# Gated delta-rule attention: state update through a weighted k, z kept token-major, three steps on other engines, and a new order on every engine

## The chip, the cores and the metric

The program runs on one core of a Trainium2 chip. A core has five engines that run their own instruction streams and meet through semaphores: TensorE (PE, matrix products; its weight loads are shown apart as PEld), VectorE (DVE), ScalarE (ACT), GpSimd (POOL) and SyncE (SP, which here only issues DMAs). The metric is the device time of one execution in microseconds (us); less is better.

## The reference

One transformer layer with eight samples of 512 tokens and 256 channels: modulation and LayerNorm, a gated delta-rule attention with 16 key heads and 32 value heads of width 128, and a mixture of experts. Nearly all time goes to the attention, which in essence is this:

```python
qkvz  = h @ W_qkvz.T                      # q, k, v go through a causal 4-tap convolution and silu; z does not
decay = tril(exp(g_i - g_j))              # g: cumulated log gates inside a chunk
T     = inverse(I - A);  A = -strict_tril((k*beta) @ k.T * decay)
for each chunk:                           # state starts at 0, one 128 x 128 matrix per value head
    v_new = T @ (v*beta) - (T @ (k*beta*exp(g))) @ state
    out   = (q*exp(g)) @ state + tril(q @ k.T * decay) @ v_new
    state = state*exp(g_last) + (k*exp(g_last - g)).T @ v_new
y = (norm_weight * (rmsnorm(out) * silu(z))) @ W_out.T
```

## The kernel before

There are three parts, one after the other: `modulation_and_gates`, `attention`, `experts`. The change lies in `attention`.

A **step** is one sample and one key head with its two value heads: 128 steps. The kernel works with chunks of 128 tokens, so a step has four chunks and eight units (chunk times value head). Each engine runs a loop whose body is written out by hand in a table (`PE_ORDER`, `ACT_ORDER`, `DVE_ORDER`, `POOL_ORDER`). An entry such as `Y2@3` means: task Y, part 2, of the step that is three ahead of the loop's count. One pass of the body does every task once, for steps up to four ahead; this software pipeline is the only thing that sets the order. Each engine takes its entries strictly in that order, and a wait that is not met holds all that stands behind it. `loop` runs the partly filled passes at the ends, and a register loop of two passes for the rest.

The tasks, with the lines of the kernel before:

- `P0` to `P11` (PE, L658): the projection, six tiles of 128 columns (k, q, v, v, z, z), two products each into two PSUM banks by turns. `C` (ACT, L886) and `T0` to `T11` (DVE, L1018): the convolution. `SK`, `SQ`, `SV`, `Z` (ACT): silu.
- `KT`, `QT`, `VT` (PE) transpose to token-major. `KN`, `QN` (ACT square, DVE sum), `PW` (POOL root) and `SM`, `SN` (DVE) give the norms' factors; `w_c` holds the weight of each token in the state update.
- `GL` (POOL, L1194): adds a constant table `bound` (0 or -1e30) to the gate rows; `GE` (ACT, L924): the decay as exp. `KK` (PE, L690), `GA` (DVE, L1072): the matrices A and attn of all units. `SL` (POOL, L1203) puts -1 on A's diagonal.
- The **ladder** inverts the 64 x 64 blocks of all eight units by doubling. A rung n is `M` (PE, L718), `q` (DVE, L1085), `Y` (PE, L725), `y` (DVE, L1093), `X` (DVE, L1102, a transpose) and `XB` (half on ACT, L936, half on POOL, L1225), and the next `Y` needs this `XB`. It begins with `AB` (DVE, L1078), `L` (PE, L713), `y0` (DVE, L1090), and has five rungs. `s`, `XD`, `Q6`, `p6` (DVE, L1113), `Z6`, `YC`, `XC` join the blocks, and `D`, `F`, `RL`, `G`, `v`, `W`, `IV` refine the inverse.
- The **state chain** of a step: `KS` (PE, L803, k against state), `RR` (DVE, L1129), `TR` (PE, L816), then `VX` (ACT, L979, the copy `vx`) and `VW` (DVE, L1140, the same product times `w_c`), `U` (PE, L826, k_tok against `vw`), `ST` (DVE, L1151), `SD` (POOL, L1239) and `O` (PE, L837 and L838).
- The end of a step: `OT`, `OQ` (ACT), `OS` (DVE), `OP`, `ON` (POOL, L1244 and L1253: the RMS factor and its product with the output), `ON` (PE, L852, a transpose), `HT` (DVE, L1164: times norm_weight and z), `OY` (PE, L868), `YA` (DVE, L1170).

SyncE loads weights and gate rows one to four steps ahead; before each load it waits for the last reader of the buffer.

Of the kernel before, what the change touches and what calls it, by code (L numbers as in the profile page):

```python
# [33 lines left out]
PE_ORDER = ("M2@3 ON1@1 O0@2 VT0@3 Y2@3 KS1@2 W1@2 M3@3 TR1@2 P0@4 Y3@3 U1@2 P1@4 M4@3 KS2@2 O1@2 P2@4 Y4@3 TR2@2 "  # L34
            "P3@4 M5@3 VT1@3 O2@2 U2@2 P4@4 KS3@2 Y5@3 P5@4 KT@4 QT@4 XD@3 Q6@3 TR3@2 P6@4 Z6@3 P7@4 D0@3 O3@2 XC@3 "
            "D1@3 KK0@4 KK1@4 P8@4 OY0@1 OY1@1 G0@3 L@4 P9@4 W0@3 M1@4 P10@4 TR0@3 Y1@4 G1@3 P11@4 U0@3 ON0@2")
ACT_ORDER = ("GE@2 OT3@0 C3@2 OQ3@0 XC@1 SV0@2 AO@2 v0@1 IV0@1 XB1@2 VX0@1 v1@1 SV1@2 XB2@2 OT0@1 Z0@2 Z1@2 XB3@2 "
             "IV1@1 VK0@2 VX1@1 C0@3 XB4@2 OT1@1 OQ0@1 VX2@1 C1@3 OQ1@1 XB5@2 OT2@1 VK1@2 OQ2@1 SK@3 SQ@3 C2@3 KN@3 "
             "QN@3 XD@2 VX3@1 KT@3 YC@2")
DVE_ORDER = ("T10@3 y0@3 T11@3 X1@3 q1@3 YA1@0 VW0@2 y1@3 X2@3 ST0@2 HT0@1 q2@3 HT1@1 y2@3 RR1@2 X3@3 q3@3 VW1@2 "  # L40
# [1606 lines left out]
```

## Time and profile before

| | before |
|---|---|
| median of 3 runs | 4839.93 us (4837.36 to 4840.07) |
| profiled execution, span from first to last instruction | 4831.3 us |
| PE busy | 4671.0 us, 97% |
| DVE busy | 4411.5 us, 91% |
| ACT busy | 3467.6 us, 72% |
| POOL busy | 2743.0 us, 57% |
| DMA engines | 377.26 MB moved, queue busy 24.7% |

The span of the profiled execution is 8.6 us under the median. Attention fills it from about 118 us to 4665 us. A matrix product's duration in the trace includes the time it takes to drain, in which the next one already runs; a busy share of PE therefore tells less than the distance from one start to the next. The same holds in a small measure on the other engines, where an instruction often starts some 0.1 us before the end of the one in front.

### The profile page before, as it was taken

To read this page: it belongs to the slowest core of one execution; us is meant where nothing else is said; L and a number is where in the kernel's file an instruction comes from. 1 tells how busy PE (TensorE), PEld (TensorE's weight loads), DVE (VectorE), ACT (ScalarE), POOL (GpSimd) and SP (SyncE) were. 2 spreads that over 40 slices of the span, in tenths; PEclk is the share of its full clock that TensorE was granted. 3 is DMA by queue.
4 is the path that set the end of the run, shared out by engine and by line. 5 is a ranking of instruction groups with operands and counts; after the bars stand their busy time and mean duration, and the time that the engine had idled before them with its cause. 6 is when DMAs were issued, how large, how long until landed. Compare 5 with 4: busy or idle time off the path is not lost. (4 is left out here: it accounts for less than half of the span.)

```text
span 4831.3 us, 132942 instructions
## 1 busy us (share of the span) xinstructions
PE 4671.0 (97%) x38533; PEld 3195.1 (66%) x38788; DVE 4411.5 (91%) x9152; ACT 3467.6 (72%) x8336; POOL 2743.0 (57%) x2329
## 2 busy tenths in 40 slices
...
DMA packets 185165, 377.26 MB, mean 78 GB/s; under 512 B 86400, under 2 KB 95744, under 8 KB 184960
## 3 DMA queue, kind: packets, MB, share of 16 engines
q1 hardware_dynamic: 185088, 376.46, 24.7%
...
q8 instruction: 20, 0.33, 0.0%
...
## 5 line engine op out<-in xcount | busy, mean ns | idle before, releaser
L658 PE MATMUL p_proj<-hid,w_in 128*128 128x512 f32 x3072 | 1626.7, 612 | 30.0 <-POOL ident_h L1185 28.9
L1018 DVE SCALAR_TENSOR_TENSOR conv<-p_proj,taps,conv 128x509 f32<-128x509 f32 (+2 forms) x1536 | 1134.8, 739 | 48.2 <-ACT conv L886 34.9
L1199 POOL TENSOR_TENSOR root<-sums,half_pow 128x8 f32<-128x8 f32 x128 | 210.8, 1647 | 862.9 <-DVE sums L1028 843.9
L1225 POOL TENSOR_SCALAR_AFFINE_SELECT x_bd<-x_t 128x512 bf16<-128x512 bf16 x640 | 422.6, 660 | 213.5 <-DVE x_t L1102 211.2
L658 PEld LDWEIGHTS p_proj<-hid,w_in 128*128 128x128 f32 x3072 | 497.3, 192 | 55.1 <-POOL ident_h L1185 29.1
L1093 DVE TENSOR_TENSOR y_h<-p_lev,y_h 128x512 bf16<-128x512 f32 x640 | 440.2, 688 | 74.4 <-PE p_lev L725 74.4
L868 PE MATMUL p_out<-h_t,w_out 128*128 128x512 f32 x1024 | 476.5, 608 | 2.2 <-DVE h_t L1164 1.1
L936 ACT ACTIVATE x_bd<-x_t 64x512 bf16<-64x512 bf16 x640 | 397.7, 621 | 96.3 <-DVE x_t L1102 96.2
L1102 DVE STREAM_TRANSPOSE x_t<-y_h 128x512 bf16<-128x512 bf16 x640 | 450.3, 704 | 4.5
L1072 DVE SCALAR_TENSOR_TENSOR ga<-p_out,neg_c,dec 128x256 f32<-128x256 f32 x1024 | 412.9, 477 | 35.4 <-ACT dec L924 34.8
L886 ACT ACTIVATE conv<-p_proj,taps 128x512 f32<-128x512 f32 x512 | 351.7, 687 | 121.9 <-PE p_proj L658 119.3
L1085 DVE TENSOR_TENSOR q_h<-p_lev,consts 128x512 bf16<-128x512 f32 x640 | 429.6, 671 | 3.8 <-PE p_lev L718 3.8
L979 ACT ACTIVATE vx<-p_b 128x256 f32<-128x256 f32 x512 | 197.9, 386 | 285.8 <-PE p_b L816 161.4
L1217 POOL TENSOR_TENSOR r_lo<-resid 128x1024 bf16<-128x1024 f32 x128 | 242.3, 1893 | 247.9 <-DVE resid L1118 247.9
L838 PE MATMUL p_b<-vx,ga 128*128 128x128 f32 x2048 | 375.1, 275 | 0.0
L868 PEld LDWEIGHTS p_out<-h_t,w_out 128*128 128x128 f32 x1024 | 184.6, 190 | 285.0 <-DVE ga L1072 147.9
L725 PEld LDWEIGHTS p_lev<-q_h,x_bd 128*128 128x128 bf16 x5120 | 216.5, 97 | 213.5 <-issue 101.5
L985 ACT ACTIVATE o_tok<-p_b 128x256 f32<-128x256 f32 x512 | 194.1, 379 | 199.5 <-PE p_b L838 196.4
L718 PEld LDWEIGHTS p_lev<-y_h,a_bd 128*128 128x128 bf16 x5120 | 222.7, 98 | 152.1 <-issue 84.2
L1232 POOL TENSOR_TENSOR q_dec<-kq,e_row 128x512 f32<-128x512 f32 x256 | 320.0, 1271 | 0.0
L924 ACT ACTIVATE dec<-low,g_neg 128x128 f32<-128x128 f32 x1024 | 313.3, 388 | 1.6
L1244 POOL TENSOR_TENSOR o_sc<-o_sc,neg_half 128x8 f32<-128x8 f32 x128 | 211.4, 1651 | 168.9 <-DVE o_sc L1159 168.9
...
## 6 DMA issues: line engine op xcount, KB each, us to landing
w_in<-in_w_in SPq DMA_DIRECT2D x128, 768.0 KB, 6.3
g_row<-rows_scratch SPq DMA_DIRECT2D x128, 512.0 KB, 3.2
hid<-h_scratch SPq DMA_DIRECT2D x128, 512.0 KB, 7.4
e_row<-exp_rows_scratch SPq DMA_DIRECT2D x128, 512.0 KB, 5.3
w_out<-in_w_out SPq DMA_DIRECT2D x128, 256.5 KB, 2.7
...
```

The costliest lines, as they stand in the source:

```text
L658: last = pe.matmul(p_proj[tile % 2][:], w_in[p][:, kt, tile * P:(tile + 1) * P], hid[p][:, kt, :], start=(kt == 0), stop=(kt == KT - 1))
L838: last = pe.matmul(p_b[:, at], ga[p][:, n * HD + h, 1, :], vx[:, h, :], start=(n == 0), stop=True)
L868: last = pe.matmul(p_out[n][:], w_out[p][:, h * D + n * P:h * D + (n + 1) * P], h_t[:, :, h, :], start=(h == 0), stop=(h == HD - 1))
L886: act.activation(conv[:, n, :], p_proj[n % 2][:], ACT.Copy, scale=taps[p][:, n, PAD:PAD + 1])\
L936: act.activation(x_bd[0:HB, :, 0:HB], x_t[0:HB], ACT.Copy).then_inc(s["xbd"], 1)
L1018: dve.scalar_tensor_tensor(conv[:, tile, late:], p_proj[tile % 2][:, 0:S - late], taps[p][:, tile, j:j + 1], conv[:, tile, late:], ALU.mul ...
L1072: last = dve.scalar_tensor_tensor(ga[p][:, u], kk, neg_c[p][:, n, h:h + 1], each(dec[:, u, :], 2), ALU.mult, ALU.mult)
L1085: dve.tensor_tensor(q_h[:], levels(), each(const["mask"][:, n * HB:(n + 1) * HB], U), ALU.mult)\
L1093: dve.tensor_tensor(y_h[:], levels(), y_h[:], ALU.add).then_inc(s["y_done"], 1)
L1102: dve.transpose(x_t[:].rearrange("p u f -> p (u f)"), y_h[:].rearrange("p u f -> p (u f)"))\
L1225: pool.affine_select(x_bd[:, :, HB:P], x_t[:], [[0, U], [0, HB]], ALU.is_ge, zero, base=-HB, channel_multiplier=1).then_inc(s["xbd_low"], 1)
L1232: last = pool.tensor_tensor(q_dec[p][:, :, h, :], kq[p][:, :, 1, :], e_row[p][:].rearrange("p (c h) i -> p c h i", h=HD)[:, :, h, :], ALU. ...
```

## The change

- **Weighted k.** `VW` is gone. A new task `KW` on POOL makes `k_w` = k_tok times `w_c` for chunks 0 to 2 and both heads, 768 elements per partition. `U` takes `vx` itself and is two products of 128 columns in place of one of 256.
- **z token-major.** `P8` to `P11` have the hidden states of one chunk as the stationary operand and 256 columns of weights as the moving one: two products of 256 columns each, where one of 512 was. `ON` on POOL gets a second instruction that multiplies the output by z. `HT` has only norm_weight left to apply; it moves from DVE to ACT as a scaled copy.
- **Half product on ScalarE.** `p6` on DVE becomes `PH` on ACT.
- **Causal bound.** `GL` is an affine_select with fill -1e30; the constant table `bound` is gone.
- **Orders.** All four tables are new, and the lists of who frees a PSUM bank follow them. Most steps are now at most three ahead, and the end of a step falls in its own pass.

```diff
-PE_ORDER = ("M2@3 ON1@1 O0@2 VT0@3 Y2@3 KS1@2 W1@2 M3@3 TR1@2 P0@4 Y3@3 U1@2 P1@4 M4@3 KS2@2 O1@2 P2@4 Y4@3 TR2@2 "
+PE_ORDER = ("U0@1 Y1@2 P11@2 O0@1 M2@2 KS1@1 P0@3 Y2@2 TR1@1 P1@3 M3@2 U1@1 O1@1 KS2@1 Y3@2 VT0@2 P2@3 TR2@1 M4@2 P3@3 U2@1 "
...
+        k_w = two("k_w", [P, NC - 1, HD, DH])
...
-                    last = pe.matmul(p_proj[tile % 2][:], w_in[p][:, kt, tile * P:(tile + 1) * P], hid[p][:, kt, :],
-                                     start=(kt == 0), stop=(kt == KT - 1))
+                    if tile < 4:
+                        ...
+                    else:
+                        c = n - 4 * KT
+                        for k in range(KT):
+                            last = pe.matmul(p_proj[tile % 2][:, kt * HD * DH:(kt + 1) * HD * DH],
+                                             hid[p][:, k, c * CH:(c + 1) * CH], w_in[p][:, k, 4 * P:6 * P],
+                                             start=(k == 0), stop=(k == KT - 1))
...
                 elif name == "U":
-                    t.wait(pe, "vw_done", n + 1)
+                    t.wait(pe, "vx_done", n + 1)
-                        t.wait(pe, "k_tok_done")
+                        t.wait(pe, "kw_done")
-                    pe.matmul(p_a[:, HD * DH:2 * HD * DH], k_tok[p][:, n, :], vw[:].rearrange("p h f -> p (h f)"),
-                              start=True, stop=True).then_inc(s["u_mm"], 1)
+                    for h in range(HD):
+                        last = pe.matmul(p_a[:, (HD + h) * DH:(HD + h + 1) * DH], k_w[p][:, n, h, :], vx[:, h, :],
+                                         start=True, stop=True)
+                    last.then_inc(s["u_mm"], 1)
...
+                elif name == "PH":
+                    t.wait(act, "q6_mm")
+                    t.wait(act, "z6_mm", back=1)
+                    act.activation(p_h[HB:P], p_lev[HB:P, :].rearrange("p (u f) -> p u f", f=HB), ACT.Copy).then_inc(s["p6_done"], 1)
...
                 elif name == "VX":
-                    if n < NC - 1:
-                        t.wait(act, "vw_done", n + 1)
+                        t.wait(act, "u_mm", n)
...
+                elif name == "HT":
+                    t.wait(act, "on_mm", n + 1)
+                    t.wait(act, "y_out", back=1)
+                    act.activation(cols(h_t, n), bank(n), ACT.Copy, scale=const["norm_w"]).then_inc(s["h_done"], 1)
...
-                elif name == "p":
-                    dve.tensor_copy(p_h[HB:P], levels()[HB:P]).then_inc(s["p6_done"], 1)
...
-                elif name == "VW":
-                    dve.tensor_tensor(vw[:], p_b[:, 0:HD * DH].rearrange("p (h f) -> p h f", h=HD),
-                                      over(w_c[p][:, n, :], [P, HD, DH]), ALU.mult).then_inc(s["vw_done"], 1)
...
-                elif name == "HT":
-                    dve.scalar_tensor_tensor(cols(h_t, n), bank(n), const["norm_w"], cols(z_t[p], n),
-                                             ALU.mult, ALU.mult).then_inc(s["h_done"], 1)
...
-                    pool.tensor_tensor(low[:], g_row[p][:], each(const["bound"], U), ALU.add).then_inc(s["g_low"], 1)
+                    pool.affine_select(low[:], g_row[p][:], [[0, U], [1, CH]], ALU.is_ge, far_below, base=0,
+                                       channel_multiplier=-1).then_inc(s["g_low"], 1)
...
+                elif name == "KW":
+                    t.wait(pool, "k_tok_done")
+                    t.wait(pool, "w_scaled")
+                    t.wait(pool, "u_mm", back=2)
+                    pool.tensor_tensor(k_w[p][:], k_tok[p][:, 0:NC - 1].unsqueeze(2).to_broadcast([P, NC - 1, HD, DH]),
+                                       w_c[p][:, 0:NC - 1].unsqueeze(3).to_broadcast([P, NC - 1, HD, DH]), ALU.mult)\
+                        .then_inc(s["kw_done"], 1)
...
                     pool.tensor_tensor(o, o, scale, ALU.mult).then_inc(s["o_nrm"], 1)
+                    t.wait(pool, "o_nrm", 1)
+                    t.wait(pool, "z_done")
+                    pool.tensor_tensor(o, o, z_t[p][:].rearrange("p c h f -> p (c h) f"), ALU.mult).then_inc(s["o_nrm"], 1)
```

POOL, before, from `XB` of rung 1 to `AL` (a_lo) in one pass of the loop; the four rows of x_bd are `XB` of rungs 1 to 4. Rows that only hold a wait or count in a register are left out here and below:

```order
L1225 AFFINE_SELECT x_bd<-x_t 128x8x64 [waits at_y_mm]
L1253 TENSOR_TENSOR o_tok<-o_tok,o_sc 128x1024 [waits at_ot_done]
L1225 AFFINE_SELECT x_bd<-x_t 128x8x64 [waits at_xt_done,at_y_mm]
L1239 TENSOR_TENSOR state_dec<-state,g_exp 128x256 [waits fed_g0]
L1194 TENSOR_TENSOR low<-g_row,consts 128x1024 [waits at_decay]
L1225 AFFINE_SELECT x_bd<-x_t 128x8x64 [waits at_xt_done,at_y_mm]
L1232 TENSOR_TENSOR q_dec<-kq,e_row 128x4x128 [waits at_o_mm,fed_e1,at_q_act]
L1232 TENSOR_TENSOR q_dec<-kq,e_row 128x4x128
L1225 AFFINE_SELECT x_bd<-x_t 128x8x64 [waits at_xt_done,at_y_mm]
L1209 TENSOR_TENSOR a_rest<-ga 128x1024 [waits at_d_mm]
L1239 TENSOR_TENSOR state_dec<-state,g_exp 128x256 [waits at_st_done]
L1213 TENSOR_TENSOR a_lo<-a_rest 128x1024 [waits at_d_mm,at_rest]
```

The same stretch now, from rung 1 to rung 4:

```order
L1224 AFFINE_SELECT x_bd<-x_t 128x8x64 [waits at_xt_done,at_y_mm]
L1259 TENSOR_TENSOR o_tok<-o_tok,o_sc 128x1024 [waits at_ot_done]
L1262 TENSOR_TENSOR o_tok<-o_tok,z_t 128x1024 [waits at_z_done,at_o_nrm]
L1245 TENSOR_TENSOR state_dec<-state,g_exp 128x256 [waits fed_g0,at_st_done]
L1224 AFFINE_SELECT x_bd<-x_t 128x8x64 [waits at_xt_done,at_y_mm]
L1231 TENSOR_TENSOR q_dec<-kq,e_row 128x4x128 [waits at_o_mm,fed_e1,at_q_act]
L1231 TENSOR_TENSOR q_dec<-kq,e_row 128x4x128
L1224 AFFINE_SELECT x_bd<-x_t 128x8x64 [waits at_xt_done,at_y_mm]
L1192 AFFINE_SELECT low<-g_row 128x1024 [waits at_decay]
L1245 TENSOR_TENSOR state_dec<-state,g_exp 128x256 [waits at_st_done]
L1208 TENSOR_TENSOR a_rest<-ga 128x1024 [waits at_d_mm,at_alo,at_strict]
L1224 AFFINE_SELECT x_bd<-x_t 128x8x64 [waits at_xt_done,at_y_mm]
```

Between rungs 1 and 2 there are now the two long products of the normalisation; q_dec, which stood before rung 4, stands before rung 3, and a_rest before rung 4 has `GL` and the second `SD` with it.

DVE, before, from the `y` of rung 4 (y_h) up to that of rung 5; conv is a tap, x_t the transpose `X`, q_h the mask `q`:

```order
L1093 TENSOR_TENSOR y_h<-p_lev,y_h 128x512 [waits at_y_mm]
L1140 TENSOR_TENSOR vw<-p_b,w_c 128x256 [waits at_u_mm,at_tr_mm]
L1102 STREAM_TRANSPOSE x_t<-y_h 128x512 [waits at_xbd_low,at_xbd,at_y_done]
L1018 SCALAR_TENSOR_TENSOR conv<-p_proj,taps,conv 128x511 [waits at_tap0]
L1085 TENSOR_TENSOR q_h<-p_lev,consts 128x512 [waits at_y_mm,at_q_mm]
L1018 SCALAR_TENSOR_TENSOR conv<-p_proj,taps,conv 128x509 [waits at_conv_done]
L1151 TENSOR_TENSOR state<-p_a,state_dec 128x256 [waits at_o_mm,at_sdec,at_u_mm]
L1018 SCALAR_TENSOR_TENSOR conv<-p_proj,taps,conv 128x510 [waits at_tap1]
L1018 SCALAR_TENSOR_TENSOR conv<-p_proj,taps,conv 128x511 [waits at_tap1]
```

DVE now, from the `y` of rung 4 to that of rung 5:

```order
L1109 TENSOR_TENSOR y_h<-p_lev,y_h 128x512 [waits at_y_mm]
L1033 SCALAR_TENSOR_TENSOR conv<-p_proj,taps,conv 128x509 [waits at_conv_done]
L1118 STREAM_TRANSPOSE x_t<-y_h 128x512 [waits at_xbd_low,at_xbd,at_y_done]
L1101 TENSOR_TENSOR q_h<-p_lev,consts 128x512 [waits at_y_mm,at_q_mm]
L1033 SCALAR_TENSOR_TENSOR conv<-p_proj,taps,conv 128x510 [waits at_tap1]
L1033 SCALAR_TENSOR_TENSOR conv<-p_proj,taps,conv 128x511 [waits at_tap1]
L1109 TENSOR_TENSOR y_h<-p_lev,y_h 128x512 [waits at_y_mm]
```

Before the `y` of rung 5 there stand six instructions now, where nine stood: vw is gone, and one tap and the state's update have moved to earlier rungs.

## Rows read from the trace of the kernel before

**Rows 1.** Busy time by engine over 58 passes; columns as the header says.

```profile
core 0: us, PE busy (x) PEld busy (x) DVE busy (x) ACT busy (x) POOL busy (x), PEclk, DMA share, GB/s
1010.93:3044.85 2033.92, 2017.70 (x17172) 1397.76 (x17286) 1940.12 (x4060) 1530.90 (x3713) 1231.63 (x1044) 1.00 0.25 77
```

**Rows 2.** PE over time: start, length, engine, line, operation, tiles, shape, count.

```profile
2403.18 0.63 PE L706 MATMUL p_out<-consts,v_t 128*128 128x128 f32 x4
2403.65 0.39 PE L837 MATMUL p_b<-state,q_dec 128*128 128x128 f32 x2
...
2404.55 0.60 PE L826 MATMUL p_a<-vw,k_tok 128*128 128x256 f32 x2
2404.98 1.02 PE L658 MATMUL p_proj<-hid,w_in 128*128 128x512 f32 x2
2405.84 0.59 PE L803 MATMUL p_a<-state,kq 128*128 128x256 f32 x2
2406.27 0.40 PE L725 MATMUL p_lev<-q_h,x_bd 128*128 128x64 bf16 x8
2406.50 1.10 PE L658 MATMUL p_proj<-hid,w_in 128*128 128x512 f32 x2
...
2411.67 0.22 PE L764 MATMUL p_out<-y_dn,ga 128*128 128x128 bf16 x1
...
2412.34 0.44 PE L837 MATMUL p_b<-state,q_dec 128*128 128x128 f32 x2
...
2417.28 3.70 PE L868 MATMUL p_out<-h_t,w_out 128*128 128x512 f32 x8
2420.82 0.39 PE L780 MATMUL p_out<-x_dn,resid 128*128 128x128 bf16 x4
```

**Rows 3.** Groups by line of what leaves DVE: count, busy us, mean ns, idle before.

```profile
L1140 DVE TENSOR_TENSOR vw<-p_b,w_c 128x256 f32<-128x256 f32 x384 | 159.7, 416 | 14.3 <-PE p_b L816 7.4
L1164 DVE SCALAR_TENSOR_TENSOR h_t<-p_out,norm_w,z_t 128x512 f32<-128x512 f32 x256 | 191.1, 747 | 8.7 <-PE p_out L852 3.3
L1113 DVE CAST p_h<-p_lev 64x512 bf16<-64x512 f32 x128 | 88.9, 694 | 4.6 <-PE p_lev L737 0.7
```

**Rows 4.** Groups by line on ACT: a scaled copy of 512, a half copy.

```profile
L886 ACT ACTIVATE conv<-p_proj,taps 128x512 f32<-128x512 f32 x512 | 351.7, 687 | 121.9 <-PE p_proj L658 119.3 <-issue 2.6
L945 ACT ACTIVATE y_dn<-p_lev 64x512 bf16<-64x512 f32 x128 | 75.8, 592 | 3.5 <-PE p_lev L743 0.3
```

**Rows 5.** Groups by line on POOL: products, selects and the root.

```profile
L1232 POOL TENSOR_TENSOR q_dec<-kq,e_row 128x512 f32<-128x512 f32 x256 | 320.0, 1271 | 0.0
L1194 POOL TENSOR_TENSOR low<-g_row,consts 128x1024 f32<-128x1024 f32 x128 | 302.3, 2362 | 0.2 <-POOL ident_h L1185 0.2
L1253 POOL TENSOR_TENSOR o_tok<-o_tok,o_sc 128x1024 f32<-128x1024 f32 x128 | 242.7, 1896 | 0.2
L1203 POOL TENSOR_SCALAR_AFFINE_SELECT ga<-ga 128x1024 f32<-128x1024 f32 x128 | 140.4, 1097 | 229.9 <-DVE ga L1072 229.9
L1199 POOL TENSOR_TENSOR root<-sums,half_pow 128x8 f32<-128x8 f32 x128 | 210.8, 1647 | 862.9 <-DVE sums L1028 843.9 <-DVE sums L1024 19.0
```

**Rows 6.** DVE and POOL over time, a transpose and its POOL half.

```profile
2426.09 0.71 DVE L1102 STREAM_TRANSPOSE x_t<-y_h 128x512 bf16<-128x512 bf16 x1
2426.99 0.66 POOL L1225 TENSOR_SCALAR_AFFINE_SELECT x_bd<-x_t 128x512 bf16<-128x512 bf16 x1 [0.51 <-DVE x_t L1102]
```

**Rows 7.** DVE over time: tap, RR, y, tap, q, tap, state, taps.

```profile
2401.04 0.74 DVE L1018 SCALAR_TENSOR_TENSOR conv<-p_proj,taps,conv 128x510 f32<-128x510 f32 x1
2401.76 0.69 DVE L1093 TENSOR_TENSOR y_h<-p_lev,y_h 128x512 bf16<-128x512 f32 x1
...
2404.55 0.73 DVE L1018 SCALAR_TENSOR_TENSOR conv<-p_proj,taps,conv 128x509 f32<-128x509 f32 x1
2405.20 0.42 DVE L1151 TENSOR_TENSOR state<-p_a,state_dec 128x256 f32<-128x256 f32 x1
2405.53 1.53 DVE L1018 SCALAR_TENSOR_TENSOR conv<-p_proj,taps,conv 128x510 f32<-128x510 f32 x2
```

118 lines of the change are left out of this document (56 added, 62 removed), and 3 rows, old and new, of the table DVE_ORDER.

## Prediction

> **What bounds the kernel now.** I read the busy time by engine first, then PE and DVE over time, then the groups by line. The middle of the attention repeats itself: [rows 1] hold 58 passes (4060 DVE instructions, 70 a pass) in 2033.92 us at a granted clock of 1.00, so a pass takes 35.07 us, and 128 of them are 4489 us of the 4831.3 us span. Everything hangs on the length of a pass. In one pass DVE is busy 1940.12/58 = 33.45 us, ACT 26.4, POOL 21.2. PE shows 34.8, but that counts drains. From start to start [rows 2] a projection pair takes 0.86 us, four transposes 0.45, a 256-column product 0.43, eight 64-column products 0.23, the four products of one O 0.90 (twice 0.45), a half of `D` 0.67, and the eight rows of `OY` 3.54. One pass of PE is then: twelve P 10.3; six transposes 2.6; `KK` 1.7; `OY` 3.5; three `KS` and three `U` 2.6; four `TR` 1.8; four `O` 3.1; fourteen groups of 64 columns 3.2; `XD` 0.5; `D` 1.3; `G` 0.4; `W` 1.8 (each half is a `D` half and an identity product of 0.21). The sum is 32.9 us. So PE waits for 2.2 us of a pass and DVE for 1.6: DVE is the bound by a hair, and PE stands right behind it. That caps what relief of DVE can give.
>
> **The change part by part.** Off DVE go three `VW`, two `HT` and `p6`: (159.7 + 191.1 + 88.9)/128 = 3.4 us a pass [rows 3]. DVE falls to 30.0 us busy, and PE with its 32.9 becomes the bound.
>
> PE's columns stay the same: `P8` to `P11` are eight products of 256 where four of 512 were, and each `U` is two of 128. The trace has no projection with 256 columns. Between the bounds of nothing (512 columns in 0.43 a row, 256 columns in 0.215, the same rate [rows 2]) and 0.06 per P as the extra weight load shows itself, I take 0.2 us a pass for both edits: floor 33.1.
>
> ACT gets two `HT`, scaled copies of 512 from PSUM like L886, 0.69 each, and `PH`, 0.59 like L945 [rows 4]: 26.4 + 2.0 = 28.4 us. No new function set comes in, all three are copies.
>
> POOL: `GL` falls from 2.36 to a select of 1024 elements, 1.10 in the row of `SL` [rows 5]. The product with z reads two full fp32 tiles, as L1194 does, so 2.36 and not the 1.90 of L1253, whose second operand is one number per 128; its other end is q_dec's 1.27 for 512, that is 2.54. `KW` has 768 elements: 1.42 by L1253's rate, to which its weight operand is nearest, 1.9 by q_dec's. I take 1.5. POOL is at 21.2 - 1.3 + 2.4 + 1.5 = 23.8 us. Sums alone say nothing against this; the orders do.
>
> The GPSIMD Engine Reference of the Trainium skill (section 4.1, Engine selection) sends elementwise products of two tensors to VectorE, since GpSimd takes about twice as long. The price agrees with the rows of L1194 and L1253; as a rule for this kernel I set it aside, since the time on POOL is only paid where somebody waits for it. Its section 1 also says that GpSimd shares its SBUF interfaces with VectorE, which would lengthen POOL's products beside DVE work; that is among the rivals.
>
> **The new orders, walked with row durations.** I follow the ring of dependences that closes after one pass. It starts at `L`, the ladder's first product.
>
> By PE, from `L` to `U1`: `L`, P9, `G1`, `W0`, M1, `W1`, `TR0`, P10, `U0`, Y1, P11, `O0`, M2, `KS1`, P0, Y2, `TR1`, P1, M3: 9.85 us by the distances above. Then `U1` 0.60, and on DVE from `ST1` on without a gap: `ST1`, T0, T1, `RR2`, y3, X4, q4, T2, `ST2`, y4, T3, X5, q5, T4, T5, up to y5. A tap takes 0.66 from start to start, 0.79 when the next needs its result, y 0.61, a state update 0.33 [rows 7], together 9.2 us. That is 19.7 from `L` to y5.
>
> By POOL, from `L`: 0.2 until `OS1` is done, root 1.65, its factor 0.3, XB1 0.63, both normalisation products 4.3, `SD` 0.6, XB2 0.65, q_dec 2.5, XB3 0.63, `GL` 1.05, `SD` 0.6, a_rest 1.85, XB4 0.65: 15.6 us [rows 5, 6]. An XB starts 0.2 after its X ends. Y4 and y4 follow, 0.4, and T3, X5, q5, T4, T5 with y4 3.95: 19.95 to y5. The two ways are equal within 0.3. What `GL` loses in length, the z product takes up; without it this way would be the bound.
>
> From y5 back to `L`: T5 ends as y5 starts; on ACT `SQ`, C2, `OT2`, `PH`, `XD`, `KT`, `QN` 4.25; the DVE sum 0.68; the root on POOL 1.85; `SM0` to `SM3` with `F1` between them 1.5; `GA` 3.2; `SL` 1.25; `AB` 0.95 with the hand-over: 13.7 us. `KW` stands before `SL` on POOL; after `F1` it and `RL` take 0.2 + 1.9 + 1.5 = 3.6 against `GA`'s 3.6, so it hides, and at 1.9 it would cost 0.3.
>
> The ring is 19.95 + 13.7 = 33.7 us. With 0.2 for the split products and 0.15 for near misses of `KW` and of Y2 behind XB2 I take **34.05 us a pass**, 1.0 over PE's floor. The waits on PE should lie before `L` (on `AB`), before `D0` (on `YC`), and at Y2 and Y4.
>
> SyncE loses nothing: the gate factors follow the same step's last `YA`, now 6 us before `SD1` needs them. The ends of the loop keep their length but for the last normalisation, with the z product of 2.4 us in the open. The other parts are unchanged; the missing table is nothing beside 377 MB.
>
> Sum: 4831.3 - 128 x (35.07 - 34.05) + 2.4 = 4703; with the 8.6 us by which the median stands over the span, 4712.
>
> **Rivals.**
>
> 1. *PE reaches its floor.* If real hand-overs are a little shorter than my ring or the slack lies elsewhere, a pass is 33.1 to 33.5: 4831.3 - 128 x 1.8 + 11 = 4612. For it: the ring exceeds the floor by only 0.6 before surcharges. Against it: PE lost 2.2 us a pass when its partner DVE was full, and four engines are dense now.
> 2. *The waits stay.* PE's 2.2 us are hand-overs of an in-order ladder and not the wait for a full DVE; then a pass is 33.1 + 1.9 = 35.0 and the time about 4840. For it: DVE too lost 1.6 us though it was the bound.
> 3. *A slower ladder.* The five rungs now stand 3.5 us apart where 2.8 is the least (y 0.69, X 0.70, a hand-over of 0.2, XB 0.66, Y and its hand-overs 0.5), and a 1.9 to 2.5 us product stands before three of the XBs on POOL. If XB3, XB4 and XB5 each miss by 0.5 more than in my walk, the pass is 35.5: 4831.3 + 128 x 0.45 + 11 = 4900. It decides from 0.35 a rung on.
> 4. *POOL's products stretch* through the shared interfaces. Eight products come to some 15 us; a tenth more puts 0.9 on the POOL way: 35.0 a pass, about 4830. Against it: they are alike in mean whether large or small [rows 5], and DVE was 95% busy beside them.
>
> **How the numbers follow.** The forecast (33.6 to 34.6 a pass, 4655 to 4785) has 0.62, rival 1 0.14, rivals 2 and 4 together 0.15, rival 3 0.09. The range of 4640 to 4795 takes in `KW` at its dear end (4750) and leaves some 0.2 outside. A difference under 0.2%, 10 us, can't be told from no change. Faster takes the forecast, rival 1 and most of the middle cases: 0.86; same 0.04; slower 0.10.
>
> **What would show it.** DVE near 30.0 us busy of a pass, POOL near 23.8, ACT near 28.4. PE's gaps should fall from 2.2 to about 1.1 us a pass, and the z product and `KW` last 2.36 and 1.4 to 1.9. The forecast is wrong if POOL is idle before each XB and the pass is still long, if ACT holds up `VX` or `XB`, or if the 256-column products run slower than 0.43 a pair.

## The result, and the profile after

The changed kernel is slower: median 5039.4 us (5038.2 to 5041.7, 4 runs) against 4838.7 us (4836.2 to 4840.1, 4 runs) in the same job, a ratio of 1.0416 [1.0401, 1.0431]. The forecast was 4712, with a range of 4640 to 4795. The profiled execution has a span of 5038.3 us.

From the windows of the changed kernel, 54 passes between two first products `L`; the columns are those of [rows 1]:

```profile
core 0: us, PE busy (x) PEld busy (x) DVE busy (x) ACT busy (x) POOL busy (x), PEclk, DMA share, GB/s
1016.57:2999.30 1982.73, 1884.45 (x16850) 1403.56 (x16850) 1769.13 (x3456) 1539.77 (x3618) 1283.01 (x1080) 1.00 0.23 73
```

A pass takes 36.72 us where it took 35.07. DVE is busy 32.8 us of it, PE 34.9, ACT 28.5, POOL 23.8. ACT and POOL are where the prediction put them (28.4 and 23.8). DVE is not: 30.0 were expected. So 2.8 us of DVE's time are something else than the work that was counted. The groups by line, of the whole execution, show 2.2 of them; the rest is taken up below. First what was priced ahead (columns as in [rows 3]):

```profile
L1262 POOL TENSOR_TENSOR o_tok<-o_tok,z_t 128x1024 f32<-128x1024 f32 x128 | 302.0, 2359 | 10.0
L1238 POOL TENSOR_TENSOR k_w<-k_tok,w_c 128x768 f32<-128x768 f32 x128 | 188.0, 1469 | 0.0
L1192 POOL TENSOR_SCALAR_AFFINE_SELECT low<-g_row 128x1024 f32<-128x1024 f32 x128 | 139.2, 1087 | 3.1 <-issue 2.7 <-POOL ident_h L1182 0.4
L1001 ACT ACTIVATE h_t<-p_out,norm_w 128x512 f32<-128x512 f32 x256 | 172.0, 673 | 10.5 <-PE p_out L859 10.5
L957 ACT ACTIVATE p_h<-p_lev 64x512 bf16<-64x512 f32 x128 | 75.8, 592 | 3.1
```

These answer [rows 4, 5]: the z product lasts 2.36 us, `KW` 1.47, the select 1.09, `HT` 0.67 and `PH` 0.59. All were as forecast. Then three groups in which the loss shows:

```profile
L1061 DVE SCALAR_TENSOR_TENSOR neg_c<-cc,inv 128x8 f32<-128x8 f32 x128 | 239.8, 1874 | 4.4
L1068 DVE TENSOR_TENSOR w_c<-neg_c,g_col 128x8 f32<-128x8 f32 x128 | 79.3, 619 | 0.0
L898 ACT ACTIVATE z_t<-p_proj 128x512 f32<-128x512 f32 x256 | 150.6, 588 | 112.1 <-POOL o_tok L1262 112.0 <-PE p_proj L664 0.2
```

`neg_c` (task `SM3`) has eight numbers per partition. In the profile before it took 21.3 us in all, 167 ns each; now it takes 1874 ns. `w_c` (`SN0`) went from 156 ns to 619. The arithmetic and the shapes of both are the same. The third line is a plain wait: `Z` on ACT waits for the second product of `ON`, 0.9 us a pass.

DVE over time in the changed kernel, start and length first:

```profile
2411.59 0.17 DVE L1049 TENSOR_SCALAR neg_n<-root 128x8 f32<-128x8 f32 x1 [0.37 <-POOL root L1198]
2411.80 0.20 DVE L1053 RECIPROCAL inv<-neg_n 128x8 f32<-128x8 f32 x1
2411.92 0.68 DVE L1130 TENSOR_TENSOR resid<-p_out,consts 128x512 f32<-128x512 f32 x1
2412.52 0.16 DVE L1058 TENSOR_TENSOR cc<-inv,g_col 128x8 f32<-128x8 f32 x1
2412.71 1.89 DVE L1061 SCALAR_TENSOR_TENSOR neg_c<-cc,inv 128x8 f32<-128x8 f32 x1
2414.79 3.23 DVE L1088 SCALAR_TENSOR_TENSOR ga<-p_out,neg_c,dec 128x256 f32<-128x256 f32 x8 [0.19 <-DVE neg_c L1061]
```

POOL over the same time:

```profile
2412.68 1.89 POOL L1216 TENSOR_TENSOR r_lo<-resid 128x1024 bf16<-128x1024 f32 x1 [1.12 <-DVE resid L1130]
2414.53 1.47 POOL L1238 TENSOR_TENSOR k_w<-k_tok,w_c 128x768 f32<-128x768 f32 x1
2418.18 1.10 POOL L1202 TENSOR_SCALAR_AFFINE_SELECT ga<-ga 128x1024 f32<-128x1024 f32 x1 [2.18 <-DVE ga L1088]
```

`neg_c` begins 0.03 us after `r_lo` and ends with it, while `r_lo` keeps its normal 1.89 us. Before, `F1` stood behind `SM3`. These rows are DVE and then POOL of the kernel before:

```profile
2414.36 0.17 DVE L1046 SCALAR_TENSOR_TENSOR neg_c<-cc,inv 128x8 f32<-128x8 f32 x1
2414.47 0.69 DVE L1118 TENSOR_TENSOR resid<-p_out,consts 128x512 f32<-128x512 f32 x1
2415.07 0.16 DVE L1052 TENSOR_TENSOR w_c<-neg_c,g_col 128x8 f32<-128x8 f32 x1
```

```profile
2415.24 1.89 POOL L1217 TENSOR_TENSOR r_lo<-resid 128x1024 bf16<-128x1024 f32 x1 [1.79 <-DVE resid L1118]
```

`neg_c` was over 0.7 us before `r_lo` started. The new order has `F1` between `SM1` and `SM2`; that releases `r_lo` just as `neg_c` is due. And `neg_c` opens `GA`, the head of the chain to `L`.

### The profile page after: what moved, and what is told of

It reads as the page before. It is cut to its first block and busy times, and to the rows that moved or that the text cites. A ratio compares the mean times of both kernels' runs of the same rounds, so it can differ in the third digit from the quotient of the medians.

```text
span 5038.3 us, 136395 instructions
## 1 busy us (share of the span) xinstructions
PE 4684.8 (93%) x40580; PEld 3441.5 (68%) x40580; DVE 4319.1 (86%) x8384; ACT 3736.8 (74%) x8718; POOL 3066.3 (61%) x2585
## 5 line engine op out<-in xcount | busy, mean ns | idle before, releaser
L659 PE MATMUL p_proj<-hid,w_in 128*128 128x512 f32 x2048 | 1110.6, 624 | 54.3 <-POOL ident_h L1182 28.8
L1109 DVE TENSOR_TENSOR y_h<-p_lev,y_h 128x512 bf16<-128x512 f32 x640 | 438.3, 685 | 260.7 <-PE p_lev L733 260.7
L664 PE MATMUL p_proj<-w_in,hid 128*128 128x256 f32 x2048 | 552.1, 392 | 1.0 <-DVE conv L1033 1.0
L1088 DVE SCALAR_TENSOR_TENSOR ga<-p_out,neg_c,dec 128x256 f32<-128x256 f32 x1024 | 412.9, 475 | 24.1 <-DVE neg_c L1061 23.8
L664 PEld LDWEIGHTS p_proj<-w_in,hid 128*128 128x128 f32 x2048 | 362.1, 192 | 35.1 <-DVE conv L1033 1.5
L659 PEld LDWEIGHTS p_proj<-hid,w_in 128*128 128x128 f32 x2048 | 310.7, 191 | 107.8 <-ACT z_t L898 73.2
L846 PEld LDWEIGHTS p_b<-vx,ga 128*128 128x128 f32 x2048 | 310.4, 192 | 6.6
L961 ACT ACTIVATE x_dn<-p_tr 64x512 bf16<-64x512 f32 x128 | 75.5, 590 | 322.3 <-PE p_tr L757 322.3
```

What stands on the lines that cost most here:

```text
L659: last = pe.matmul(p_proj[tile % 2][:], w_in[p][:, kt, tile * P:(tile + 1) * P], hid[p][:, kt, :], start=(kt == 0), stop=(kt == KT - 1))
L664: last = pe.matmul(p_proj[tile % 2][:, kt * HD * DH:(kt + 1) * HD * DH], hid[p][:, k, c * CH:(c + 1) * CH], w_in[p][:, k, 4 * P:6 * P], st ...
L846: last = pe.matmul(p_b[:, at], ga[p][:, n * HD + h, 1, :], vx[:, h, :], start=(n == 0), stop=True)
L1088: last = dve.scalar_tensor_tensor(ga[p][:, u], kk, neg_c[p][:, n, h:h + 1], each(dec[:, u, :], 2), ALU.mult, ALU.mult)
L1109: dve.tensor_tensor(y_h[:], levels(), y_h[:], ALU.add).then_inc(s["y_done"], 1)
```

## The experiments

The theory: a DVE instruction of certain forms can't run while POOL runs a large one; it is held to the end. The rivals: `F1`'s place costs by itself; `Z`'s new wait; PE or POOL bind anyway. Each kernel was run against the kernel before on the same chip. Pass lengths are the distance between first products `L` near 1000 and 3000 us of the trace, divided by the number of passes.

**1. `F1` behind `SM3`, in the changed kernel**

```diff
-SM0@3 SM1@3 F1@2 SM2@3 SM3@3 GA0@3
+SM0@3 SM1@3 SM2@3 SM3@3 F1@2 GA0@3
```

> The changed kernel with one entry of DVE_ORDER moved: F1 (the residual of the inverse, whose end releases r_lo on POOL) stands behind SM3 (neg_c) in place of between SM1 and SM2. Theory A, the held instruction: neg_c reads two SBUF tensors and is held for the whole of POOL's r_lo (1.89 us for 8 elements, where the same line took 0.17 before). Out of r_lo's way it takes 0.17 again, GA starts some 1.5 us earlier, and a pass of 36.72 us falls to 35.1 to 35.4, the time to 4830 to 4875 us. Theory B, the ladder: five rungs 3.5 us apart and z's release (ScalarE waits 0.88 us a pass for the second product) set the pass; neg_c only uses slack. Then the pass moves by less than 0.4 us and the time stays above 4985 us, whatever neg_c takes.

Measured: 4847.8 us (9 runs), ratio 1.0028 [1.0018, 1.0038]; `neg_c` 167 ns, a pass 35.22 us. One entry of one table brings back 191.6 us of the 200.7 lost.

**2. `F1` between `SM1` and `SM2`, in the kernel before**

```diff
-F0@3 SM0@4 SM1@4 SM2@4 SM3@4 F1@3 SN0@3
+F0@3 SM0@4 SM1@4 F1@3 SM2@4 SM3@4 SN0@3
```

> The kernel before with F1 moved forward between SM1 and SM2, the place it has in the changed kernel, and nothing else. Theory A: r_lo now starts as neg_c does, neg_c goes from 0.17 to about 1.9 us, on an engine that was full: the pass goes from 35.07 to 36.4 to 36.9 us and the time to 5010 to 5070 us. Theory B: nothing holds neg_c here since the new tasks on POOL and the new ladder are absent; the time stays within 20 us of before.

Measured: 5039.9 us (4 runs), ratio 1.0418 [1.0401, 1.0436]; a pass 36.69 us. The same move alone makes the kernel before as slow as the changed one. Its POOL and DVE over time:

```profile
2411.51 1.90 POOL L1217 TENSOR_TENSOR r_lo<-resid 128x1024 bf16<-128x1024 f32 x1 [1.72 <-DVE resid L1118]
2411.54 1.89 DVE L1046 SCALAR_TENSOR_TENSOR neg_c<-cc,inv 128x8 f32<-128x8 f32 x1
```

**3. z product first, in the changed kernel.** The two products of `ON` change places, and `Z` waits only for the first.

```diff
-pool.tensor_tensor(o, o, scale, ALU.mult); t.wait(pool, "z_done"); pool.tensor_tensor(o, o, z)
+t.wait(pool, "z_done"); pool.tensor_tensor(o, o, z); pool.tensor_tensor(o, o, scale, ALU.mult)
-t.wait(act, "o_nrm", back=2)
+t.wait(act, "o_nrm", 1, back=2)
```

> The changed kernel with the two products of the normalisation on POOL exchanged: times z first, then times the RMS factor, and z's silu on ScalarE waits for the first alone. z_t is free 1.9 us earlier. If the wait of ScalarE for z_t (0.88 us a pass) and the projection's wait behind it (0.4 to 0.6) are part of the loss, the wait goes, the first rungs start earlier and the pass falls by 0.3 to 0.6 us: 4960 to 5000 us. If theory A alone sets the pass, 5020 to 5040 us.

Measured: 5031.2 us (4 runs), ratio 1.0402 [1.0385, 1.0419]; a pass 36.64 us. `Z`'s idle time falls from 112 us to 0.4, but the kernel gains 8 us at most, and the intervals of the two ratios (1.0401 to 1.0431 without the edit) overlap: the wait was real and stood beside the chain.

**4. Both, and `w_c` (`SN0`) right behind `SM3`**

```diff
-SM0@3 SM1@3 F1@2 SM2@3 SM3@3 GA0@3 ... ST0@2 SN0@3 X2@3
+SM0@3 SM1@3 SM2@3 SM3@3 SN0@3 F1@2 GA0@3 ... ST0@2 X2@3
```

> The changed kernel with F1 behind neg_c, w_c (SN0, held 0.35 us by POOL's z product) right behind neg_c, and the z product first. Theory A and the z release together take back 1.65 + 0.35 + 0.4 us a pass: 34.3 us, near the ring of 34.05 us of the prediction, and 4720 to 4770 us, below both kernels. If the ladder itself is the bound (theory B), 4950 us or more.

Measured: 4827.3 us (10 runs), ratio 0.9982 [0.9972, 0.9992]; `neg_c` and `w_c` 167 ns, a pass 35.01 us. Faster than the kernel before by 0.2%, but 0.7 us a pass over what I expected. So these three edits take back the whole loss against the kernel before, and experiment 1 alone takes back most of it; that the gain did not come has other causes (experiments 7, 8 and 12). One of them is a new held instruction: `OS` part 0 (`o_sc`, eight elements, two SBUF inputs) now falls beside `KW` and takes 372 ns in the median, where it took 156 in the changed kernel. DVE, then POOL:

```profile
2414.91 0.37 DVE L1159 TENSOR_TENSOR o_sc<-o_ss,q_s 128x8 f32<-128x8 f32 x1
```

```profile
2413.79 1.47 POOL L1238 TENSOR_TENSOR k_w<-k_tok,w_c 128x768 f32<-128x768 f32 x1
```

**5. `neg_c` with one SBUF input.** In the changed kernel, four `tensor_scalar` of two columns each.

```diff
-dve.scalar_tensor_tensor(neg_c[p][:], cc[:], -1.0, inv_k, ALU.mult, ALU.mult)
+for c in range(NC):
+    dve.tensor_scalar(neg_c[p][:, c, :], cc[:, c, :], inv[:, 0, c:c + 1], -1.0, ALU.mult, ALU.mult)
```

> The changed kernel with its orders as they are (F1 between SM1 and SM2, r_lo released just before neg_c), only that neg_c is made by four tensor_scalar instructions of 2 columns each with one SBUF tensor input (the factor 1/norm comes as a per-partition scalar) instead of one with two. Theory (a DVE instruction with two SBUF tensor inputs is held while a two-input POOL product runs): the four are not held, together 0.4 to 0.6 us, so GA starts 1.3 us earlier than in the changed kernel, 34.9 to 35.3 us a pass, 4815 to 4865 us. Rival (it is the place of F1 that costs, for instance that neg_c waits for r_lo's memory or that the ladder is late for another reason): 5025 to 5045 us, and one of the four lasts 1.5 us.

Measured: 5367.6 us (4 runs), ratio 1.11 [1.1081, 1.1118]. The expectation failed: the kernel got slower still. DVE, then POOL:

```profile
2410.66 3.58 DVE L1062 TENSOR_SCALAR neg_c<-cc,inv 128x2 f32<-128x2 f32 x4
```

```profile
2410.63 1.89 POOL L1217 TENSOR_TENSOR r_lo<-resid 128x1024 bf16<-128x1024 f32 x1 [1.12 <-DVE resid L1131]
2412.48 1.47 POOL L1239 TENSOR_TENSOR k_w<-k_tok,w_c 128x768 f32<-128x768 f32 x1
```

The four end 0.3 us behind `k_w`. A `tensor_scalar` on fp32 in SBUF is held as well. The records of the four are 1890, 1512, 216 and 215 ns, nearly the same in 127 of 128 steps: the first is held to the end of `r_lo`, the second starts 0.02 us before `k_w` and is held to its end, and the last two are free. A pass is 39.29 us. That is 2.6 us more than in the changed kernel, of which these rows explain 1.7; the rest was not followed up. It was not `F1`'s place alone that costs, and "two inputs" was too narrow.

**6. Small DVE instructions beside known POOL instructions.** On the kernel of experiment 4, results unread.

```diff
+GA0, then tensor_scalar 128x8, then tensor_tensor 128x8   (r_lo runs)
+T8, then tensor_tensor 128x8                             (root runs)
+T9, then tensor_tensor 128x8                             (SL runs)
+q5, then tensor_tensor 128x8                             (XB5 runs)
+q1, then tensor_copy 128x128, then tensor_tensor 128x8   (z product runs)
```

> The kernel with all three order changes (F1 late, w_c right behind neg_c, z product first), plus small DVE instructions of 128x8 on constants, whose results nobody reads. Beside r_lo (two full tensors, 1.9 us): first one with one input, then one with two. Behind T8, beside the root (pow of 128x8 on POOL, 1.65 us): two inputs. Behind T9, beside SL (affine select of 1024 fp32, 1.1 us): two inputs. Behind q5, beside XB5 (select of 512 bf16, 0.66 us): two inputs. Behind q1, beside the product with z (2.37 us): a copy of 128x128 fp32, then two inputs. Theory: 'two SBUF inputs are held to the end of a POOL instruction with two inputs': one input 0.17 us, the copy 0.2 us; beside r_lo about 1.2 us, beside z 0.5 to 1.2 us, beside the root 1.2 us; beside the two selects 0.17 us. Rival a: any POOL instruction holds: SL up to 0.5, XB5 up to 0.4 us too. Rival b: only large ones hold: 0.17 us beside the root. Rival c: anything on DVE that reads SBUF is held: the copy and the one-input instruction too. The time is of no interest: some 0.5 to 2 us more a pass.

Measured, groups by line; L1051 and L1041 stand beside `r_lo`, L1043 beside the root, L1045 beside `SL`, L1047 beside `XB5`, L1053 and L1049 beside the z product:

```profile
L1053 DVE COPY junk<-consts 128x128 f32<-128x128 f32 x128 | 168.7, 1318 | 0.0
L1051 DVE TENSOR_SCALAR junk<-consts 128x8 f32<-128x8 f32 x128 | 165.4, 1292 | 0.0
L1045 DVE TENSOR_TENSOR junk<-consts 128x8 f32<-128x8 f32 x128 | 80.9, 632 | 0.0
L1047 DVE TENSOR_TENSOR junk<-consts 128x8 f32<-128x8 f32 x128 | 46.8, 366 | 0.0
L1043 DVE TENSOR_TENSOR junk<-consts 128x8 f32<-128x8 f32 x128 | 19.9, 156 | 0.0
L1049 DVE TENSOR_TENSOR junk<-consts 128x8 f32<-128x8 f32 x128 | 19.7, 154 | 0.0
L1041 DVE TENSOR_TENSOR junk<-consts 128x8 f32<-128x8 f32 x128 | 19.6, 153 | 0.0
```

Selects hold too (0.63 and 0.37 us to their ends), and a copy and a `tensor_scalar` are held: rival a is right for the selects, and part of rival c. Those that come behind a held one (L1041, L1049) take 153 and 154 ns; they start as one POOL instruction ends and just before the next begins. Beside the root nothing is held (156 ns), as rival b said, although the root lasts 1.64 us. The time was 5032 us (one run), a pass 36.65 us, 1.6 more than in experiment 4.

**7. Half of `OY` left out,** on the kernel of experiment 4: `for h in range(1)`, the second head's part of the output projection.

> The kernel with all three order changes (4827 us, 35.0 us a pass), where OY leaves out the second head's product: four instead of eight matmuls of 512 columns, 1.7 us less of PE's work in each pass, in the stretch from y5 to L where PE stands beside the chain of squares, root, neg_c, GA, SL, AB. It leaves out half of the output projection. Theory 'the ring through GA binds there': L waits for a_bd as before, 4800 to 4830 us. Rival 'PE's own sequence binds' (its distances add up to 34.6 us here and not to the 32.9 us of the estimate): 1.7 us a pass less at most, 4620 to 4700 us. Between them: both are equally long, then the gain is a few tenths a pass.

Measured: 4816.2 us (5 runs), ratio 0.9962 [0.9948, 0.9976]. 1.7 us less of PE's work a pass brought 11 us in all. PE's waits before `L`, in experiment 4 and then in experiment 7:

```profile
L721 PE MATMUL p_lev<-eye_h,a_bd 128*128 128x64 bf16 x1024 | 51.8, 194 | 12.6 <-DVE a_bd L1094 12.6
```

```profile
L788 PE MATMUL p_out<-x_dn,resid 128*128 128x128 bf16 x1024 | 99.0, 219 | 73.4 <-DVE y_acc L1167 73.4
L721 PE MATMUL p_lev<-eye_h,a_bd 128*128 128x64 bf16 x1024 | 52.5, 195 | 51.9 <-DVE a_bd L1094 51.9
```

PE now waits for `YA` (0.6 us in experiment 4) and `a_bd` instead: the chain through `GA` closes that half of the ring.

**8. Half of `P9`, `P10` and `P11` left out,** on the kernel of experiment 4 (one of two products in each sum).

> The kernel with all three order changes (4827 us), where P9, P10 and P11 leave out the second half of their sum: 2 instead of 4 matmuls of 256 columns each, together 1.3 us less of PE's work in a pass, all between L and U1, where PE has hardly a gap. It leaves out half of the z and part of the projection sum. Theory 'the ring's half from L to U1 is PE's own sequence': a pass gets shorter by what PE saves until the way by POOL (o_tok products, q_dec, XB3) binds: 0.5 to 1.2 us a pass, 4675 to 4765 us. Rival 'POOL's way already binds there' : 4800 to 4830 us.

Measured: 4817.7 us (5 runs), ratio 0.9962 [0.9948, 0.9976], against 1.3 us less of PE's work a pass. The ladder's `Y`, in experiment 4 and then in experiment 8:

```profile
L733 PE MATMUL p_lev<-q_h,x_bd 128*128 128x64 bf16 x5120 | 253.3, 193 | 3.7 <-POOL x_bd L1224 2.9
```

```profile
L734 PE MATMUL p_lev<-q_h,x_bd 128*128 128x64 bf16 x5120 | 253.3, 193 | 65.0 <-POOL x_bd L1225 63.8 <-ACT x_bd L944 1.1
```

The 61 us more are POOL's: its way (products of `ON`, q_dec, `XB`) is nearly as long as PE's. My first theory for this half was wrong, the rival right.

**9. Three exchanges on the kernel of experiment 4**

```diff
 ACT   -KT@3 QN@3              +QN@3 KT@3
 POOL  -PW@3 RL@2 KW@2 SL@3    +PW@3 KW@2 RL@2 SL@3
 DVE   -YA0@0 AB0@3 AB1@3 OS1@1   +YA0@0 OS1@1 AB0@3 AB1@3
```

> The kernel with all three order changes (4827 us, 35.0 us a pass), with three more exchanges of neighbours on the two halves of the ring. From y5 to L: QN before KT on ACT (squares 0.4 us earlier, so the root too), KW before RL on POOL (SL no longer waits 0.2 us for KW, and OS0 no longer 0.2 us), OS1 before AB0 on DVE (0.1 us on that way). From L to y5: the power on POOL starts 0.8 us earlier by OS1's new place. Theory: both halves are closed by chains without slack (14.6 us from y5 to L, 20.4 us from L to y5 by POOL and by PE alike); halving OY or P9 to P11 did not help since another chain stood beside. Then y5 to L gets 0.3 to 0.5 us shorter and L to y5 at most 0.1: 34.5 to 34.7 us a pass, 4760 to 4790 us. Rival: the chain of y5 to L ends on PE's own sequence (OY's last product), so nothing comes of it: 4815 to 4830 us. Second rival: an exchange brings a held instruction back (OS1 beside SL, or the sum beside another product): over 4840 us.

Measured: 4932.8 us (5 runs), ratio 1.0203 [1.0189, 1.0217]: the second rival in kind, a held instruction, but with a victim that it did not name. `KW` now starts as the root ends, exactly when `SM0`, a `tensor_scalar`, wants to start. DVE, then POOL:

```profile
2427.73 1.39 DVE L1049 TENSOR_SCALAR neg_n<-root 128x8 f32<-128x8 f32 x1
```

```profile
2426.03 1.64 POOL L1198 TENSOR_TENSOR root<-sums,half_pow 128x8 f32<-128x8 f32 x1 [6.15 <-DVE sums L1043]
2427.63 1.47 POOL L1238 TENSOR_TENSOR k_w<-k_tok,w_c 128x768 f32<-128x768 f32 x1
```

1390 ns in place of 171: I walked into the same trap again, with its rule half known.

**10. `neg_c` on ACT,** in the changed kernel, orders as they are but for the new entry `NC` behind `VX3`.

```diff
-dve.scalar_tensor_tensor(neg_c[p][:], cc[:], -1.0, inv_k, ALU.mult, ALU.mult)
+for c in range(NC):
+    act.activation(neg_c[p][:, c, :], cc[:, c, :], ACT.Copy, scale=inv[:, 0, c:c + 1])
```

> The changed kernel with its orders, r_lo released at the same place, only that neg_c is made on ACT: four scaled copies of 128x2 (the sign goes into cc on DVE), on an engine that does not share its SBUF access with POOL. Theory (DVE instructions whose tensors are all in SBUF are held to the end of the POOL instruction that runs; ACT's are not): the four take about 0.2 us each beside r_lo, GA starts 0.8 to 1.1 us earlier than in the changed kernel: 35.3 to 35.8 us a pass, 4860 to 4930 us. Rival (r_lo's release itself, or F1's place, costs): 5025 to 5045 us, or ACT's instructions last over 1 us beside r_lo.

Measured: 4898.9 us (4 runs), ratio 1.0137 [1.0122, 1.0153]; a pass 35.61 us. ACT over time, and POOL:

```profile
2413.33 0.85 ACT L959 ACTIVATE neg_c<-cc,inv 128x2 f32<-128x2 f32 x4 [1.99 <-DVE cc L1066]
```

```profile
2413.31 1.90 POOL L1220 TENSOR_TENSOR r_lo<-resid 128x1024 bf16<-128x1024 f32 x1 [1.12 <-DVE resid L1134]
```

The same arithmetic at the same moment beside the same `r_lo` is not held on ACT. So it is DVE's instruction that is held while POOL's runs, and not `r_lo`'s release that costs.

**11. More forms.** On the kernel of experiment 4: behind `GA0` a `reduce_sum` (128x128 to 4), a `reciprocal` (128x8) and a copy from fp32 to bf16 (128x128), behind `q1` a product of two bf16 inputs (128x8).

> The kernel with all three order changes, plus small DVE instructions on constants, to see which forms are held. Beside r_lo, in this order: a reduce_sum of 128x128 fp32 to 4, a reciprocal of 128x8 fp32, a copy of 128x128 from fp32 to bf16. Beside the product with z: a product of two bf16 inputs of 128x8. So far held: two SBUF inputs (fp32), a tensor_scalar and a copy with one fp32 SBUF input; not held: anything with a PSUM input, and the 32x32 transposes of bf16. Theory 1 (held are two SBUF inputs, and forms that DVE runs at a multiple of its rate): the sum 0.2 us and not held, the reciprocal not held, the copy held for what is left of r_lo, the bf16 product held. Theory 2 (held is everything with all tensors in SBUF but the transposes): the sum is held, about 1.1 us.

```profile
L1044 DVE TENSOR_TENSOR junk_b<-ident_h 128x8 bf16<-128x8 bf16 x128 | 161.6, 1262 | 0.0
L1042 DVE CAST junk_h<-consts 128x128 bf16<-128x128 f32 x128 | 133.8, 1045 | 0.0
L1038 DVE TENSOR_REDUCE junk<-consts 128x4 f32<-128x128 f32 x128 | 35.2, 275 | 0.0
L1040 DVE RECIPROCAL junk<-consts 128x8 f32<-128x8 f32 x128 | 24.6, 192 | 0.0
```

Theory 1: the sum and the reciprocal run free, the copy and the bf16 product are held (4955.8 us, one run).

**12. An order that keeps such instructions clear of POOL,** from experiment 4: `KW` in POOL's idle stretch between `XB5` and the root, `SD1` behind `XB2`, `QN` and `OS1` as in experiment 9.

```diff
 POOL  -SD1@1 XB2@2   +XB2@2 SD1@1
 POOL  -XB5@2 PW@3 RL@2 KW@2 SL@3   +XB5@2 KW@2 PW@3 RL@2 SL@3
```

> The kernel with all three order changes (4827 us, 35.0 us a pass), with four exchanges that keep every DVE instruction of a form that was held away from POOL's large instructions. On POOL KW stands between XB5 and the root, where POOL was idle for 6.5 us and DVE runs taps and y5 from PSUM (so SL no longer waits 0.2 us for it, and no held instruction follows the root), and SD1 stands behind XB2 (XB2 0.6 us earlier). On ACT QN stands before KT (squares 0.4 us earlier). On DVE OS1 stands before AB0, behind SL. Theory: the chain from y5 to L loses 0.3 to 0.5 us, the one from L to y5 0 to 0.2 us, no instruction is held over 0.3 us: 34.5 to 34.8 us a pass, 4765 to 4805 us. Rival: PE's own sequence is at its end in both halves (98.8% busy): 4815 to 4830 us. Second rival: KW beside DVE's q_s or y_dn copies behind y5 holds them: 0.3 to 1 us a pass more, 4860 to 4950 us.

Measured: 4813.4 us (5 runs), ratio 0.9955 [0.9941, 0.9968]: faster than both kernels, by 0.45% and by 4.5%. A pass is 34.91 us, no small instruction of DVE is held (`neg_n` 161 ns, `neg_c` 166, `w_c` 166), and PE is busy 1986 of 2000 us. It is nearly the first rival's time: only 0.1 us a pass of the 0.3 to 0.5 came. One reason is that `GA`, which had no idle time at all in experiment 4, now waits for `KK` on PE:

```profile
L1088 DVE SCALAR_TENSOR_TENSOR ga<-p_out,neg_c,dec 128x256 f32<-128x256 f32 x1024 | 412.8, 475 | 33.0 <-PE p_out L697 33.0
```

That is 0.26 us a pass: the shorter chain of norm factors ran up against PE.

## Why the prediction was wrong

**The step that failed** is the term "`SM0` to `SM3` with `F1` between them 1.5" in the way from y5 back to `L`. In the timeline above, `SM0` starts at 2411.59 and `GA` at 2414.79: 3.20 us, with 1.72 of them in `neg_c`. From y5 (2404.45) to `L` (2420.26) it is 15.81 us where 13.7 were summed. The other terms: to the end of the sum 5.25 (4.93 summed), root 1.89 (1.85), `GA` 3.23 (3.2), `SL` 1.26 (1.25), `AB` 0.98 (0.95). So 1.7 of the 2.1 us too much in this half is one instruction of eight elements. 1.71 us times 128 are 218 us; experiments 1 and 2 put the step's worth at 192 and 204 us.

**The other half of the ring** was summed too short as well: from `L` to the next y5 it takes 20.9 us (2420.26 to 2441.13) and not 19.95. Three rows of the changed kernel, of PE, DVE and POOL, show where:

```profile
2431.11 0.69 PE L835 MATMUL p_a<-vx,k_w 128*128 128x128 f32 x4
2432.03 0.42 DVE L1154 TENSOR_TENSOR state<-p_a,state_dec 128x256 f32<-128x256 f32 x1
2428.44 0.66 POOL L1224 TENSOR_SCALAR_AFFINE_SELECT x_bd<-x_t 128x512 bf16<-128x512 bf16 x1 [0.32 <-DVE x_t L1118]
```

PE reaches `U1` 10.85 us after `L` where 9.85 were summed, and DVE starts `ST1` at 11.8 and not at 10.45. From there to y5 DVE has no idle time and needs 9.1 us, as summed (9.2). POOL is not in front: XB4 ends 16.35 us after `L` where 15.6 were walked, but POOL waits 0.3 us for DVE's transpose before XB2 and again before XB4. The held `w_c` stands right before the first of these transposes. With `w_c` free and the z product first (experiment 4) this half takes 20.4 us.

**DVE's 30.0 us** were too low by themselves. `neg_c` and `w_c` are 2.2 of the 2.8 us. In experiment 4, where both take 167 ns, DVE is still busy 31.0 us a pass, 0.2 of it `o_sc`. The prediction took off the full lengths of six instructions, though instructions on DVE overlap their neighbours by some 0.1 us each; that this is the rest is argued and not shown.

**Why it was missed.** I priced each instruction by its row before, and [rows 5] only for the price of POOL's products. Which DVE instruction would stand beside which POOL product I did not ask, though the move of `F1` changed just that. One sign lay in the trace of before: `o_sc` (L1156, two SBUF inputs) took 156 ns at least and 712 at most.

**Rival 4** had the shared interface but the wrong victim: it let POOL's products stretch. They did not (1.89 and 2.36 us, beside held instructions too). The one who came second waited for the rest of the other's instruction, and that was DVE. The price was then set by the length of POOL's instruction and not by a share. The prediction had taken the rule from a table of the GPSIMD Engine Reference of the Trainium skill. The page SBUF — State Buffer of the Trainium skill, section "Who interferes with whom", says more: a vector instruction that reads two tensors from SBUF contends with a GpSimd instruction that reads SBUF, and so does one in a two-port mode, which copies, casts and `tensor_scalar` can enter. Whoever comes first has the ports for its whole instruction, and "the other **fully blocks** (not throttle)"; `tensor_reduce` and ScalarE are never concerned. The runs agree form by form: held are 1874 ns for two inputs, 1292 for `tensor_scalar`, 1318 for a copy, 1045 for a cast; not held are the sum (275), ACT's copies (284 each), and `GA`, which reads PSUM (475 ns beside `r_lo`, 477 before). One GpSimd instruction does not fit the page: the root reads two tensors from SBUF and holds nobody (156 ns, experiment 6), and there the measurement decides. By that page `neg_c`, due 0.03 us after `r_lo`'s start, would have been priced at about `r_lo`'s length, which is what it took.

**The second miss** was the edge from `Z` to the second product of `ON`: 0.9 us a pass of wait on ACT that was not in the walk. It cost 8 us at most (experiment 3).

**With `neg_c` and `w_c` free** the forecast would still have been wrong: 35.01 us a pass (experiment 4), not 34.05. In that kernel the two halves measure 14.6 us (y5 at 2402.90, `L` at 2417.51) and 20.4 us (next y5 at 2437.90), against 13.7 and 19.95. This is not one cause but pieces of 0.2 to 0.3 us each: in the first half the squares on ACT end at +4.5 and not +4.25, `w_c` takes 0.2, `SL` waits 0.2 for `KW`, and `AB` starts 0.28 us after `SL` has ended. This last piece is mostly the held `o_sc`: it pushes the tap and the `YA` in front of `AB` back by 0.2 us. The time here is rival 2's ("the waits stay", 35.0 us, about 4840). Its reason fits too: experiments 7 and 8 took 1.7 and 1.3 us off PE, and each gave under 0.1 us a pass, since PE's, POOL's and `GA`'s ways are nearly equally long. DVE's 3.4 us had gone off an engine that no longer closed the ring once the others stood still.

**Right were** the engines' sums for ACT and POOL, the three POOL prices, and the 256-column products: a P of four lies 0.86 to 0.95 us from the next start, with no idle time of its own (L664: 1.0 us in all). Rival 1 (the floor, 33.1) is out: no kernel came under 34.9. PE's real distances are longer than the shortest ones that I had added up to 32.9 from [rows 2]. Rival 3 (late `XB`s) did not make the loss. The ladder of the changed kernel, y1 to y5, took 15.0 us (2426.13 to 2441.13) where four rungs of 3.5 are 14.0; that is 0.25 a rung, under the 0.35 from which rival 3 was to decide, and the kernel before takes 16.7. DVE's waits for `Y`, 260.7 us where there were 74.4, come to 1.5 us a pass more, but they are 271.4 us in experiment 4, which is 212 us faster. The extra 1.0 us is still part of what the other half took too long, and the rungs are uneven: 3.7, 4.6, 2.9 and 3.9 us in the mean of the middle, the longest with a state update, two taps and an `RR` of DVE right before its `y`.

**Left open:** experiment 12 shortened several pieces and gained 0.1 us a pass. `GA`'s new wait for `KK` points to PE's own sequence (99.3% busy in it) in the half from y5 to `L`; whether PE is the last bound in the other half too was not separated.
